# Pool's split of the gates behind its second wait of a step, and a wait for the first expert's one-hot in step 7

## What is computed

```python
x = x + conv_ref(ln_c(x), conv_w, conv_b)       # x * sigmoid(conv(max, mean) + b)
t = to_tokens(x)
# ffn_ref on ln_t(t):
router_probs = softmax(x @ router_w + router_b)
top_p, top_i = top_k(router_probs, 2)
top_p = top_p / sum(top_p)
expert_out = einsum('bnd,edc->bnec', x, expert_w) + expert_b
t = t + einsum('bnk,bnkc->bnc', top_p, take_along_axis(expert_out, top_i))
```

## Time and profile before

| | |
|---|---|
| time, median of 3 runs | 1416.53 us (1415.92 to 1417.59) |
| the profiled execution | 1415.82 us, span 1414.0 us |
| PE busy | 1310.5 us, 93% of the span |
| DVE busy | 1267.5 us, 90% |
| ACT busy | 1052.3 us, 74% |
| POOL busy | 1055.1 us, 75% |
| chain that ended last, by engine | PE 67%, DVE 14%, issue 8%, ACT 2% |
| mean granted clock of PE | 0.96 |

### The profile page before, as it was taken

How to read it: one execution, slowest core, us unless ns; L and a number is a source line. 1 busy time by engine, 2 the same in 40 slices (tenths; PEclk the granted TensorE clock), 3 DMA queues, 4 the chain that set the end, 5 groups by cost and what they waited for, 6 DMA issues and landing times.

```text
span 1414.0 us, 33097 instructions
## 1 busy us (share of the span) xinstructions
PE 1310.5 (93%) x11750; PEld 620.3 (44%) x11750; DVE 1267.5 (90%) x1527; ACT 1052.3 (74%) x3950; POOL 1055.1 (75%) x643
## 2 busy tenths in 40 slices
PE   8865989999899998999899998999989998999998
PEld 8864434444344443444344443444434333333332
DVE  6787899989999899998989899998999988998887
ACT  5678878888799897988888887998879644444442
POOL 6335686778678786777958777787867779787985
PEclk9955999999999999999999999999999999999999
DMA  6442556767567675576666666676756556656774
GB/s 223 131 139 58 167 172 197 211 189 213 171 184 222 187 212 177 171 234 193 188 194 198 197 202 184 190 211 195 205 171 187 158 163 169 186 161 186 206 207 145
DMA packets 85845, 259.97 MB, mean 184 GB/s; under 512 B 13744, under 2 KB 13744, under 8 KB 85680
## 3 DMA queue, kind: packets, MB, share of 16 engines
q1 hardware_dynamic: 85680, 257.85, 61.3%
HBM read 206.42 MB, written 51.38 MB: 182 GB/s over the span
## 4 chain that ended last, share of the span: by engine, by line
PE 67%; DVE 14%; issue 8%; ACT 2%; POOL 0%; DVEq 0%; ACTq 0%; POOLq 0%
PE moe L571 40%; PE tm L496 10%; PE gb L517 9%; DVE gx L717 8%; PE tm L556 2%; PE tm L510 2%; PE moe L565 2%; PE tm L595 1%; DVE stats L694 1%; DVE ge L739 1%; DVE u L842 1%; DVE ot L730 1%; ACT sq L1004 1%; DVE oh L764 1%; DVE early_s L694 1%
## 5 line engine op out<-in xcount | busy, mean ns | idle before, releaser
L571 PE MATMUL moe<-gx,wc 128*64 128x448 f32 x3584 | 814.1, 558 | 0.0
L717 DVE TENSOR_TENSOR gx<-gb,xd 128x896 f32<-128x896 f32 x672 | 710.4, 1085 | 80.1 <-PE gb L517 73.3
L1249 POOL TENSOR_TENSOR gx<-gs,xd 128x896 f32<-128x896 f32 x224 | 469.6, 2096 | 231.9 <-ACT gs L1042 207.3
L1004 ACT ACTIVATE sq<-xct 112x64 f32<-112x64 f32 x1400 | 338.3, 245 | 8.5 <-DVE early_s L704 2.1
L1042 ACT ACTIVATE gs<-gb 128x896 f32<-128x896 f32 x224 | 205.2, 916 | 185.4 <-PE gb L517 179.2
L571 PEld LDWEIGHTS moe<-gx,wc 128*64 128x64 f32 x3584 | 222.6, 137 | 207.6 <-issue 165.3
L1004 ACT ACTIVATION_READ_ACCUMULATOR sq<-xct 112x1 f32 x1400 | 265.3, 190 | 0.0
L1266 POOL TENSOR_TENSOR tt<-xc,a1s 128x896 f32<-128x896 f32 x112 | 237.4, 2120 | 6.2 <-issue 4.5
L517 PE MATMUL gb<-s,cg 32*128 32x448 f16 x1792 | 177.5, 363 | 64.7 <-DVE gx L717 62.8
L517 PEld LDWEIGHTS gb<-s,cg 32*128 32x128 f16 x1792 | 48.1, 91 | 395.8 <-DVE gx L717 357.2
L496 PE MATMUL tm<-rhs,xa 64*112 64x74 f32 x2800 | 190.0, 278 | 10.6 <-ACT logit_mean L989 5.4
(11 more groups left out here) (95 smaller groups left out, 1119.5 us busy)
## 6 DMA issues: line engine op xcount, KB each, us to landing
xd<-in_x_dram SPq DMA_DIRECT2D x448, 224.0 KB, 4.0
xa<-in_x_dram SPq DMA_DIRECT2D x112, 448.0 KB, 4.3
xc<-in_x_dram SPq DMA_DIRECT2D x112, 448.0 KB, 4.5
out_dram<-ot SPq DMA_DIRECT2D x112, 448.0 KB, 3.4
gx<-in_const_g_dram SPq DMA_DIRECT2D x1, 384.0 KB, 5.4
cf<-in_const_f_dram SPq DMA_DIRECT2D x1, 333.5 KB, 2.8
cf<-in_L_ffn_expert_b_dram SPq DMA_DIRECT2D x12, 1.0 KB
gx<-in_L_ffn_expert_w_dram SPq DMA_DIRECT2D x1, 128.0 KB, 5.2
```

The source lines that it names most:

```text
L571: last = pe.matmul(moe[b * CH:(b + 1) * CH, c, 0:HALF], wc[:, k * CH:(k + 1) * CH], gx[:, u, b, :], start=False, stop=(k == KT - 1), skip_ ...
L717: dve.tensor_tensor(gx[:, i, :, :], gb[:, 2 * slot:2 * slot + 2, 0:HALF], xd[:, v % 2, :, c * HALF:(c + 1) * HALF], ALU.mult).then_inc(sca ...
L1004: last = act.activation(sq[:, n, :], xct[:, step % 2, n, :], ACT.Square, accum_out=to[:, 1, lo + n:lo + n + 1])
L1249: pool.tensor_tensor(gx[:, ND + j, :, :], gs[:, j, :, :], xd[:, v % 2, :, j * HALF:(j + 1) * HALF], ALU.mult).then_inc(scaled_p, 1)
```

## The change

Two edits. In vector_place, Pool's wait for the end of a place of the router holds for all places in round 8 as before, and now also for place 15 in every round up to 8. Pool calls vector_place from round 2 on, so this is new in rounds 2 to 7: in step 7 Pool waits for oh1_0. In Pool's body, rest_one for v + 2 moves from ahead of the router's operations to behind vector_place of the step's second place, and stays ahead of router_tail.

```diff
-            if r == PAIRS and place in HALF_END:
+            if place in HALF_END and (r == PAIRS or place == 15) and r <= PAIRS:
                 b_done(eng, r, B_DVE, HALF_END[place])
```

```diff
                     if cur:
                         vector_place(pool, r, 2 * step)
                         scale_unit(r, v, 1)
-                    if parting:
-                        rest_one(r, v + 2)
                     if Bp:
                         router(r, step)
                     if ahead:
                         vector_place(pool, r, 2 * step + 1)
+                    if parting:
+                        rest_one(r, v + 2)
                     if tail:
                         router_tail(r - 1, step)
                     if ahead:
                         scale_unit(r, v + 1, 0)
                         scale_x(r, v + 1)
```

## The result

The changed kernel takes 1427.28 us as a median of 4 runs (1426.29 to 1428.04), against 1416.84 in the same runs: a ratio of 1.0074, with an interval of 1.0056 to 1.0091. It is 10 us slower, where 35 us faster was forecast. Its profiled span is 1424.9 us (1414.0 before).

The account below looks back on a forecast made before the run. Bound: Vector's one-hot stalled behind Pool in step 7, rounds 2 to 7. From 1415.8 us, 6 x 7.2 = 43.2 removed, 6 x (1.05 + 0.3 + 0.1) = 8.7 added, net 34.5; median 0.7 higher; forecast 1381.5, range 1370 to 1402.

Parts of the forecast that it names:

- The stall of the one-hot costs 7.2 us a round, and Pool's wait removes it: Step 7, rounds 2 to 7: Pool's wait lets L764 end about 0.5 us after L1296, removing 43.2 us in all.
- Pool is 1.0 us later from step 4 to step 7; L739 will be issued 0.3 to 0.45 us after L1249's start: Step 4's moved split no longer fills Pool's idle time, so Pool runs 1.0 us later and L739 meets L1249 early.
- Step 6, L739 is let in at L1249's end, 1.05 us a round: Step 6: L1249 ends at 689.0, L739 goes in there and ends 1.0 us later, TensorE behind it; cost 1.05 us.
- the starvation: Rival, step 6: L739 fails until Pool falls idle, 7.9 us, some 10 with slow clock; 1430 to 1436 us; chance 0.14.
- its 2.4 us for the slow clock: Step 6 rival: TensorE's slow clock adds 2.4 us to L739's 7.9 us delay, some 10 us a round.
- Steps 1 and 2 cancel, step 4 costs 0.3: L842 gains about 1.0 us in step 1, lost again by L754 in step 2 (0.8); L842 in step 4 costs 0.3.
- The turn of step 6 waits 0.1 to 0.2 us: Turn from step 5 to 6: the later split ends at 682.85, TensorE waits 0.1 to 0.2 us; taken as 0.1.
- The rule of the Trainium skill: Shared SBUF read interface of Vector and GpSimd: second comer blocks until the first's instruction ends; by it starvation cannot occur.
- The range: 1370 to 1402 us for the whole kernel, leaving out starvation and the tail of the other rivals, under 0.2.
- the rival of small collisions: L754 in step 2, L842 in step 1 or step 7's tie key waits longer: 1389 to 1408 us, chance 0.17.

Follow-up runs that it names:

- wait_only: Kernel before the change plus only Pool's wait for the one-hot in step 7 of rounds 2 to 7, split not moved: 1378.13 us, ratio 0.9724.
- moved_in_7: Changed kernel, wait kept, but the split moved in step 7 alone: 1374.51 us, ratio 0.9703.
- late_steps_moved: Changed kernel, but the split moved in steps 4 to 13 only: 1416.56 us, ratio 0.9998.
- map_phase: wait_only plus Pool memsets of about 0.3 to 1.0 us ahead of step 6's second unit, a different length in each of rounds 2 to 7: 1391.65 us.
- map_fine: map_phase with memsets of 0.76 to 0.86 us in steps of 0.02 over rounds 2 to 7: 1387.01 us.
- queue_done_2nd: Changed kernel, step 4's split kept ahead, memsets before step 6's L1249, and an already fulfilled wait (place 12's maximum) between L1288 and the split: 1409.88 us.
- queue_wait_2nd: Changed kernel, step 4's split kept ahead, memsets before step 6's L1249, and Pool's wait for L739 between L1288 and the split: 1392.31 us.
- queue_wait_3rd: As queue_wait_2nd, but the wait for L739 stands one operation later, between the split and the L1249 behind it: 1387.87 us.
- wait_13_too: Changed kernel plus Pool's wait for place 13 (L739) in rounds 2 to 7, behind L1288 and ahead of the split: 1392.73 us, ratio 0.9825.
- hot_wait_last: Kernel before the change plus Pool's wait for the one-hot behind L1266 of step 7: 1416.83 us, ratio 1.0002.
- hot_wait_mid: Kernel before the change plus Pool's wait for the one-hot between L1249 and L1266 of step 7: 1395.37 us, ratio 0.9852.
- map_halves: map_phase with step 6's second unit on Pool in two instructions, one for each image: 1387.12 us.
- after_halves: Changed kernel with step 6's second unit on Pool in two instructions, one for each image: 1398.71 us, ratio 0.9868.

## Why the prediction was wrong, point by point

- *The stall of the one-hot costs 7.2 us a round, and Pool's wait removes it*: right. wait_only gained 40 us where 43 less 6 was due (its split still stands ahead of L1296, 1.0 us in each of six rounds), and the one-hot ended 0.5 us after L1296. moved_in_7 gained 42.3.
- *Pool is 1.0 us later from step 4 to step 7; L739 will be issued 0.3 to 0.45 us after L1249's start*: right, 0.44.
- *Step 6, L739 is let in at L1249's end, 1.05 us a round*: this step failed. It was let in 4.7 us later, after three more operations of Pool. TensorE's clock fell there as it had in step 7, and the exchange came out even (late_steps_moved, 0.9998). The case stood among the rivals with a chance of 0.14. The lag was foreseen rightly, but that this phase still gets in was taken from thin evidence. I weighed failures at 0.23 us against a success at 0.63 and overlooked a nearer one in the same trace, L739 itself in step 6 of round 8: issued 0.53 us into L1249 with 1.57 us left, and let in at its end (POOL, then DVE, of before). In that round Pool's queue also holds its wait for place 13, which later proved to matter, so even this instance was no proof for rounds 2 to 7.

```profile
1180.81 2.10 POOL L1249 TENSOR_TENSOR gx<-gs,xd 128x896 f32<-128x896 f32 x1
1182.85 1.88 POOL L1255 TENSOR_TENSOR parts<-q,parts 112x448 f16<-112x448 f32 x1
...
1181.34 2.52 DVE L739 TENSOR_TENSOR ge<-lg,top 112x896 bf16<-112x896 f32 x1
```

  The rival's price was too high as well, 3 us a round for the exchange instead of 0: I let the starvation last until Pool fell idle (7.9 us longer, measured 5.6), and its 2.4 us for the slow clock come from no row, where the earlier trace rows give 7.75 - 5.8, about 2.
- *Steps 1 and 2 cancel, step 4 costs 0.3*: a mis-sized term. The move in steps 0 to 3 costs 10.7 us. L842's gain of 1.0 us in step 1 and L754's loss of 0.8 in step 2 came as forecast (1.06 and 0.82). But I followed L842 alone; the operation that needs its result, L845, was not in the sum, and its 1.78 us behind L1266 turn the two steps into a loss of 1.5 us in round 5. L842 in step 4 took the 1.1 us forecast.
- *The turn of step 6 waits 0.1 to 0.2 us*: right. From the last matmuls ahead of it to the turn takes 0.89 us after and 0.80 before (PE, round 5, after and then before; the earlier trace rows have the turn of before at 682.77):

```profile
688.75 0.97 PE L571 MATMUL moe<-gx,wc 128*64 128x448 f32 x4
689.64 0.58 PE L510 MATMUL tm<-cg,parts 112*64 112x112 f16 x16
```
```profile
681.97 0.97 PE L571 MATMUL moe<-gx,wc 128*64 128x448 f32 x4
```

  The weight loads show a wait of 0.70 us for the split, but matmuls run in most of it, and only 0.09 us reach them:

```profile
689.64 0.44 PEld L510 LDWEIGHTS tm<-cg,parts 112*64 112x64 f16 x16 [0.70 <-POOL parts L1255]
```

- *The rule of the Trainium skill*, "SBUF — State Buffer", Who interferes with whom, that the one that comes second blocks until the first's instruction ends: it gives the duration of every instance that was let in at the first handover (2.44 us in map_phase is 1.49 of waiting and 0.95 of work). By it the starvation could not occur, neither in step 7 before nor in step 6 after; the measurements decide against it for those twelve instances.
- *The range and the sums*: the range, 1370 to 1402, left the starvation out. Two sums don't come out as written. The terms give 1382.0 (1415.8 + 0.7 - 34.5) and not 1381.5, and the rival of small collisions, with 16 to 30 us added to what is left after 43, ends at 1403 and not 1408. Neither bears on the miss.

## What to carry to other kernels

When an edit shifts one engine by a microsecond against another, look for every operation of the second that the first can hold up, and for the whole chain behind it, not only for the one that the edit is about. A stall that depends on phase can be cured in its own place (wait_only) and come up in another as soon as an edit shifts the phase: try the parts of such a change one by one, since here the first alone gave -40 us, the second alone +10, and both together +10. Where a Vector operation must not be starved, let Pool stand in a wait for it instead of counting on a gap.

## What the runs showed of the hardware

- A Vector operation with two inputs in SBUF can be passed over at several handovers between Pool's instructions: 6.41 us for the one-hot, 7.31 and once 9.35 us for L739, whose own work is some 1.1 us.
- For L739 the first handover was missed when 1.60 us or more were left of Pool's running instruction and met at 1.59 or less (map_fine; at 1.59 it was also missed once, in queue_done_2nd), unless an unfulfilled wait stood two or three instructions on in Pool's queue (1.64 to 1.80 us left and let in, eight instances of eight in queue_wait_2nd and queue_wait_3rd, and 1.64 to 1.67 in six of six in wait_13_too). A fulfilled wait had no such effect. The one-hot, with 1.85 to 1.88 us left, didn't follow this (hot_wait_last, hot_wait_mid). Why is open.
- L845 was let in at L1266's end with 1.9 us left of it in the changed kernel (2.16 to 2.17 us in six rounds); there Pool's next operation, L1249, waits for L845 itself.
- Two instructions of Pool in place of one, each half as long, remove the failure in step 6 (map_halves, after_halves).
